# The MLP of a fused transformer layer as half-array matmuls through the scores' banks, and a first batch whose embedding is summed tile by tile

## The reference

```python
B, S, E = 4, 512, 1024                      # batches, positions, width
h = sum over 8 shards of W[s][clip(x - 1575*s, 0, 1574)] + 8*bias + pos_emb
qkv = layernorm(h) @ w_qkv.T                # 32 query heads, 8 key/value heads, 128 wide
probs = softmax(causal(q k^T / sqrt(128)))
h = h + (probs @ v) @ w_dense.T
t = layernorm(h)[:, perm].reshape(-1, 16, 64)          # 16 heads of 64
t = gelu(einsum('bhd,hdm->bhm', t, up))                # 64 -> 256, per head, exact gelu
out = h + einsum('bhm,hmd->bhd', t, down).reshape(-1, 1024)[:, unperm]
```

## Time and profile before

| | us |
|---|---|
| median of 3 runs (lowest to highest) | 2775.52 (2774.55 to 2777.88) |
| the profiled execution: its time | 2776.71 |
| its span on the core | 2774.9 |
| TensorE matmul busy | 2656.9 |
| ScalarE, VectorE, GpSimd busy | 1333.4, 1304.2, 1035.6 |

### The profile page before, as it was taken

How to read it: one execution, slowest core, us unless ns; L and a number is a source line. 1 busy time by engine, 2 the same in 40 slices (tenths; PEclk the granted TensorE clock), 3 DMA queues, 4 the chain that set the end, 5 groups by cost and what they waited for, 6 DMA issues and landing times.

```text
span 2774.9 us, 36350 instructions
## 1 busy us (share of the span) xinstructions
PE 2656.9 (96%) x13040; PEld 2192.2 (79%) x13040; DVE 1304.2 (47%) x3181; ACT 1333.4 (48%) x3209; POOL 1035.6 (37%) x822
## 2 busy tenths in 40 slices
PE   3999999999999999999999999999999999999988
PEld 2788888888878888887887888888787888888863
DVE  4444444554544444455453544446445445444441
ACT  2544444444455555445445555544545555554422
POOL 3333334333244444433334444443333444443311
PEclk9999999999999999999999999999999999999999
DMA  5222224222222222522222223342232222222230
GB/s 131 64 70 73 69 76 119 80 71 71 87 77 83 89 79 77 143 69 69 89 74 74 88 80 91 94 112 76 61 99 73 77 80 88 81 87 73 72 114 31
DMA packets 116556, 229.85 MB, mean 83 GB/s; under 512 B 13837, under 2 KB 13837, under 8 KB 116282
## 3 DMA queue, kind: packets, MB, share of 16 engines
q1 hardware_dynamic: 108954, 202.36, 24.6%
q0 software_dynamic: 7424, 25.17, 3.6%
HBM read 210.70 MB, written 16.78 MB: 82 GB/s over the span
## 4 chain that ended last, share of the span: by engine, by line
PE 87%; ACT 6%; DVE 4%; issue 1%; DMA 1%; POOL 0%; SPq 0%; ACTq 0%; DVEq 0%; POOLq 0%
PE fb L413 22%; PE fb L415 22%; PE fb L414 22%; PE tp L432 4%; PE sc L413 2%; PE sc L414 2%; PE sc L415 2%; PE pv L415 2%; PE pv L413 2%; PE pv L414 2%; ACT w_hi L592 1%; PE fb L469 1%; PE fb L571 1%; PE sc L423 1%; PE fb L564 1%
## 5 line engine op out<-in xcount | busy, mean ns | idle before, releaser
L882 POOL TENSOR_TENSOR w_lo<-w_raw,w_hi 128x512 fp32r<-128x512 f32 x688 | 883.1, 1303 | 1452.8 <-ACT w_hi L592 1451.3
L413 PE MATMUL fb<-xn_hi,w_hi 128*128 128x512 f32 x1536 | 607.7, 396 | 20.1 <-ACT g_raw L683 8.8
L592 ACT ACTIVATE w_hi<-w_raw 128x512 fp32r<-128x512 f32 x688 | 410.7, 631 | 408.2 <-PE fb L415 378.0
L415 PE MATMUL fb<-xn_hi,w_lo 128*128 128x512 f32 x1536 | 600.1, 391 | 0.0
L414 PE MATMUL fb<-xn_lo,w_hi 128*128 128x512 f32 x1536 | 599.7, 390 | 0.0
L413 PE MATMUL fb<-at_hi,w_hi 128*128 128x512 f32 x992 | 393.4, 397 | 8.2 <-DVE hacc L784 6.1
L608 ACT ACTIVATE prob<-sc,neg_max 128x128 f32<-128x128 f32 (+3 forms) x512 | 263.4, 527 | 282.2 <-DVE neg_max L743 281.3
L415 PE MATMUL fb<-at_hi,w_lo 128*128 128x512 f32 x992 | 387.6, 391 | 0.0
L414 PE MATMUL fb<-at_lo,w_hi 128*128 128x512 f32 x992 | 386.5, 390 | 0.0
L413 PEld LDWEIGHTS fb<-xn_hi,w_hi 128*128 128x128 f32 x1536 | 288.8, 188 | 91.6 <-ACT g_raw L683 14.0
L415 PEld LDWEIGHTS fb<-xn_hi,w_lo 128*128 128x128 f32 x1536 | 288.7, 188 | 62.1
(11 more groups left out here) (141 smaller groups left out, 3836.7 us busy)
## 6 DMA issues: line engine op xcount, KB each, us to landing
w_raw<-in_w_qkv SPq DMA_DIRECT2D x384, 256.0 KB, 2.8
w_raw<-in_w_dense SPq DMA_DIRECT2D x256, 256.0 KB, 2.6
h_tok<-in_pos SPq DMA_DIRECT2D x16, 512.0 KB, 5.6
h_rows<-hacc SPq DMA_DIRECT2D x32, 256.0 KB, 2.5
w_raw<-in_w_up SPq DMA_DIRECT2D x24, 256.0 KB
w_raw<-in_w_down SPq DMA_DIRECT2D x24, 256.0 KB, 2.5
end_up<-in_w_up SPq DMA_DIRECT2D x8, 256.0 KB, 5.1
end_down<-in_w_down SPq DMA_DIRECT2D x8, 256.0 KB, 5.2
```

The lines of the kernel that those rows point to most:

```text
L413: pe.matmul(dst, a_hi, b_hi, start=first, stop=False)
L415: return pe.matmul(dst, a_lo, b_hi, start=False, stop=last)
L592: act.activation(w_hi[:, m % RW, :], w_raw[:, m % RAW, :], copy).then_inc(w_rounded, 1)
L882: pool.tensor_tensor(w_lo[:, m % RW, :], w_raw[:, m % RAW, :], w_hi[:, m % RW, :], ALU.subtract)\
```

## The change

- In the loop the MLP no longer uses `product`. `mlp_w` holds raw f32 weights of a pair, up and down side by side (128x512, one DMA for each pair, issued by SP at step F). U is one plain f32 matmul over 64 partitions (one head, one half of the rows of the array), heads taking turns; O is four plain f32 matmuls with 64 output columns, heads taking turns between the lower and upper 64 partitions of one `fb` bank. The steps R, `y_hi`, `y_lo`, `g_hi`, `g_lo`, and the 48 weight tiles of up and down with their `w_hi` and `w_lo`, are gone.
- U's results go to the three banks of `sc` (the scores') in turn, no longer to `fb`; scores wait for the Gelus before them, a pair's first U for the exponentials before it. In the unit's order the four U stand in two groups of two.
- The end: the same forms; U goes through six banks (`sc`, `tp`, `pv`).
- The start: positions go to `first_pos` (in the space of `at_hi`/`at_lo`), the gathers don't wait for them and no longer add by DMA; POOL adds the positions tile by tile (step J); TensorE adds `h_tok` into the bank by an identity matmul; DVE takes statistics from the bank and ACT copies it back. Edge rows are loaded from ACT's queue, `coef` is made for batch 0 first and for the rest after K, statistics and scales are taken tile by tile, normalised tiles take turns in `row_buf` and `prob`, and the first eleven weight splits move from ahead of START into the X steps and Q0.

```diff
-MLP = ("S0 N0 Q2 q D0 Ta0 f D1 Tb0 S1 N1 Q3 D2 Ta1 D3 Tb1 S2 p F D4 D5 N2 D6 r D7 u0 PV0 u1 Ta2 u2 Q0 u3 Tb2 S3 P N3 "
-       "PV1 o R K Ta3 U0 PV2 U1 Tb3 U2 Q1 U3 V PV3 VT")
+MLP = ("S0 N0 Q2 q D0 Ta0 f D1 Tb0 S1 N1 Q3 D2 Ta1 D3 Tb1 S2 p F D4 D5 N2 D6 D7 u0 u1 PV0 u2 u3 Ta2 Q0 Tb2 S3 P N3 "
+       "PV1 o K U0 U1 Ta3 PV2 U2 U3 Q1 Tb3 V PV3 VT")
-START = "A G0 G1 G2 G3 B0 B1 B2 B3 B4 B5 B6 B7 La Lb X0 X1 X2 X3 X4 X5 X6 X7 Q0 K Q1 V VT"
+START = ("A G0 G1 G2 G3 J0 J1 J2 J3 B0 B1 La0 B2 Lb0 B3 La1 B4 Lb1 X0 X1 B5 La2 B6 Lb2 X2 X3 B7 La3 Lb3 X4 X5 X6 X7 "
+         "Q0 K Q1 V VT")
+        for m in range(RW):
+            first = Step("X", 0, 0, min(m // 2 * 2 + 1, 7)) if m < 8 else Step("Q", 0, 0, 0)
+            self.splits[first].append(m)
+        def up_bank(s):
+            if s.kind == "U":
+                return sc[:, (4 * PAIRS * s.b + s.i) % 3, :]
+            return (sc[:, 0, :], sc[:, 1, :], sc[:, 2, :], tp[:, 0, :], tp[:, 1, :], pv[:, :])[s.i % 6]
+            positions(first_pos)
...
+                if s.kind == "F":
+                    n = PAIRS * s.b + s.i
+                    if n > 1:
+                        sp.wait_ge(job_full, full(Step("O", (n - 2) // PAIRS, 0, (n - 2) % PAIRS)))
+                    sp.dma_start(mlp_w[:, n % 2, :], w_mlp[s.i]).then_inc(mlp_in[n % 2], 16)
...
+                if tally.ups[s] > 0:
+                    pe.wait_ge(g_done, tally.ups[s])
                 pe.matmul(sc[:, 0, 0:P], q_first[:, q, :], k_first[:, :], start=True, stop=True)
...
+            def up(dst, w, weight, rows, done):
+                own, cols = slice(DH * (w % 2), DH * (w % 2) + DH), slice(w // 2 * P, w // 2 * P + P)
+                pe.matmul(dst, weight[own, cols], rows[own, :], start=True, stop=True).then_inc(done, 1)
+            def down(s, ready, before, weight, act_of):
+                dst = start_job(s)
+                for w in range(4):
+                    h, m = w % 2, w // 2
+                    pe.wait_ge(ready, before + w + 1)
+                    at = MH + (2 * h + m) * DH
+                    mm = pe.matmul(dst[h * DH:(h + 1) * DH, :], weight[:, at:at + DH], act_of(w),
+                                   start=m == 0, stop=m == 1)
                 mm.then_inc(job_full, 1)
...
+                    if s.b == 0:
+                        pe.wait_ge(h_placed, c + 1)
+                        mm = pe.matmul(dst, ident[:, :], h_tok[:, c, half * S:(half + 1) * S], start=False, stop=True)
...
+                    if w == 0:
+                        pe.wait_ge(mlp_in[n % 2], 16 * (n // 2 + 1))
+                        pe.wait_ge(scaled, n + 1)
+                        pe.wait_ge(exp_done, 4 * tally.scores[s])
+                    if tally.ups[s] > 2:
+                        pe.wait_ge(g_done, tally.ups[s] - 2)
+                    up(up_bank(s), w, mlp_w[:, n % 2, :], y[:, n % 2, :], up_full)
...
+                elif s.kind == "B" and s.b == 0:
+                    act.wait_ge(h_stats, s.i + 1)
+                    act.activation(h_tok[:, c, half * S:(half + 1) * S], fb[:, bank(s), :], copy)\
+                       .then_inc(bank_free[bank(s)], 1)
...
-                    act.activation(g_raw[:, w % 2, :], fb[:, bank(s), :], ACT.Gelu).then_inc(bank_free[bank(s)], 1)
-                    act.activation(g_hi[:, w, :], g_raw[:, w % 2, :], copy).then_inc(g_rounded, 1)
+                    act.wait_ge(up_full, 4 * n + w + 1)
+                    act.activation(g[:, w, :], up_bank(s), ACT.Gelu).then_inc(g_done, 1)
...
+                    if s == Step("K", 0, 0, 0):
+                        dve.wait_ge(x_row_in, 64)
+                        coefficients(S, B * S).then_inc(coef_rest, 1)
...
+                elif s.kind == "J":
+                    pool.wait_ge(pos_in[s.i], 16)
+                    pool.wait_ge(gathered[s.i], 16)
+                    pool.tensor_tensor(h_tok[:, s.i, :], h_tok[:, s.i, :], first_pos[:, s.i, :], ALU.add)\
+                        .then_inc(h_placed, 1)
```

More of the change, by code:

```diff
@@ L170, in __init__, with tower_kernel @@
             self.splits[STEPS[place]].append(m)
-def tower_kernel(nc, x_cols, x_row, table, bias, pos, edge_cols, w_qkv, w_dense, w_up, w_down, perm_cols, out):
+        self.ups, self.scores, ups, scores = {}, {}, 0, 0
+        for s in STEPS:
+            self.ups[s], self.scores[s] = ups, scores
+            ups += s.kind == "U"
+            scores += s.kind == "S"
+        self.la = {s: n for n, s in enumerate(s for s in STEPS if s.kind == "La")}
+def tower_kernel(nc, x_cols, x_row, table, bias, pos, edge_cols, w_qkv, w_dense, w_mlp, perm_cols, out):
     scratch = nc.dram_tensor("h1_rows", [E, S], F32).ap()
-    weights = {"qkv": w_qkv, "dense": w_dense, "up": w_up, "down": w_down}
+    weights = {"qkv": w_qkv, "dense": w_dense}
     tally = Tally()
@@ L301, in tower_kernel @@
         selected = sem("selected")
[L302 to L304 removed]
+        coef_rest = sem("coef_rest")
+        pos_in = [sem(f"pos_in{c}") for c in range(TT)]
+        gathered = [sem(f"gathered{c}") for c in range(TT)]
+        h_placed = sem("h_placed")
+        h_stats = sem("h_stats")
+        h_moments = sem("h_moments")
+        var_step = sem("var_step")
+        shift_done = sem("shift_done")
         rstd_done = sem("rstd_done")
@@ L369, in _ @@
                 sp.dma_start(edge_consts[at, :], edge_cols).then_inc(const_in, 16)
[L370 to L381, removed]
+                token_row(at, 0, S, const_in)
+            positions(first_pos)
             for m in range(RAW):
                 load(m)
-            for m in range(RW):
-                sp.wait_ge(w_ready, m + 1)
-                load(m + RAW)
+            sp.dma_start(perm[:, :], perm_cols).then_inc(x_row_in, 16)
+            for part in range(3):
+                token_row(slice(32 * part, 32 * part + 32), S, B * S, x_row_in)
             for s in STEPS:
@@ L391, in _ @@
                     sp.wait_ge(job_full, full(Step("O", s.b - 2, 0, PAIRS - 1) if s.b > 1 else Step("H", 0, 0, 7)))
-                    for c in range(TT):
-                        sp.dma_start(h_tok[:, c, :], pos[c * P:(c + 1) * P, :]).then_inc(pos_in, 16)
+                    positions(h_tok)
                 if s.kind == "D" and s.g == G - 1:
@@ L533, in _ @@
                     dst = start_job(s)
-                    pe.matmul(dst, ones[:, :], hp[:, 0, :] if s.i else y_raw[:, :], start=True, stop=True)\
+                    pe.matmul(dst, ones[:, :], hp[:, 0, :] if s.i else y[:, 0, :], start=True, stop=True)\
                         .then_inc(job_full, 1)
@@ L588, in _ @@
             copy = ACT.Copy
+            act.wait_ge(zeroed, 1)
+            shards = table.rearrange("(s v) e -> s v e", v=VS)
+            n = SHARDS - 1
+            for part in range(3):
+                at = 32 * part
+                act.dma_start(row_buf[at:at + n, :], shards[0:n, VS - 1, :]).then_inc(edge_in, 16)
+                act.dma_start(row_buf[at + n:at + 2 * n, :], shards[1:SHARDS, 0, :]).then_inc(edge_in, 16)
+                act.dma_start(row_buf[at + 2 * n:at + EDGE, :], bias.partition_broadcast(SHARDS)).then_inc(edge_in, 16)
             def split(m):
@@ L819, in _ @@
+                    dve.bn_stats(stats[:, c, half, :], at if s.b > 0 else fb[:, bank(s), :]).then_inc(h_stats, 1)
                     if half == 1:
-                        dve.wait_ge(h_step, 15 * s.b + (3 * c + 2))
-                        dve.sem_inc(apart, 1)
-                        dve.bn_aggr(moments[:, c, :], stats[:, c, :, :]).then_inc(h_step, 1)
+                        dve.wait_ge(h_stats, 8 * s.b + s.i + 1)
+                        dve.bn_aggr(moments[:, c, :], stats[:, c, :, :]).then_inc(h_moments, 1)
```

281 lines of the change are left out of this document (124 added, 157 removed).

## The result

The changed kernel takes 2689.99 us (median of three runs, 2688.89 to 2691.08) against 2775.52 before: a ratio of 0.969, 95% interval 0.967 to 0.971, 85.5 us less. The forecast was 2718, 57.5 less, with a range of 2672 to 2770. So sign and range held, and the gain was half as large again as forecast. The profiled span is 2689.3 us against 2774.9.

What follows compares the result with a forecast made beforehand. TensorE, busy 96% and carrying 87% of the chain that ended last, was taken as the bound. 2776.7 - 24 (loop) - 19 (start) - 14 (end) = 2719.7 us profiled, 2718.5 against the median; predicted 2718, range 2672 to 2770.

Steps and rivals of the forecast that it cites:

- Slots: Loop, U and O on TensorE: half-array matmuls overlap partly, 11 slots of 0.43 us a pair, 4.75 us.
- the forecast's main case: Loop and end: half pairs, with changes between whole and half array priced; 2700 to 2735 us, chance 0.42.
- rival 2: Loop and end: full pairs, each half streaming by itself, 8 slots, 4.45 us a pair with changes; 2679 us, chance 0.17.
- Changes of form: Loop, TensorE: six changes a pair between whole and half array, 0.165 us each, 1.0 us a pair.
- The stall removed: Loop, the four U: 1.2 us of stall a pair, on an `fb` bank still held by Gelu, goes away.
- New waits in the loop: Loop: U's waits for exponentials and scores' waits for Gelus cost nothing; U3's Gelu wait bounded at 1 us for each of 12 units.
- Start: Start, batch 0: Q0 at about 41.5 us instead of 60.69, 19 us earlier; gain 15 to 25.
- End: End part, 8 pairs: a pair takes 5.8 us instead of 7.68, 14 us saved in all.
- Rival 5: End part: the clock might fall to the low level, +4 us a pair, 2749 us; chance 0.10 shared with start unmoved.

Runs made afterwards that it cites:

- experiment 1: Changed kernel with both U matmuls of a group in the same half of the array and O's four in order A, A, B, B: 2733.97 us.
- experiment 2: Changed kernel with U and O as plain f32 matmuls over the whole array, 128 rows and 128 columns, as many of them, heads mixed: 2763.0 us.
- experiment 3: Changed kernel with O placed behind K, directly ahead of the U group, in the MLP units: 2689.71 us.
- experiment 4: Changed kernel with GpSimd's adds of the positions in the start cut to one column, so the first batch lacks nearly all its positions: 2680.91 us.
- experiment 5: Changed kernel with the positions added by VectorE instead of GpSimd, the last two tiles between the first sums, nothing left out: 2682.64 us.

## Why the prediction was right, and where it was not

**Slots: the step that failed.** "The next matmul, in the other half, is behind them both and can start only beside the second": 11 slots a pair, 4.75 us. The records show eight: both halves' first records start together, and in experiment 1 even when two matmuls of the other half stand between. The row that led there (every record starts after the one before it in the program) held only because every matmul of before used the whole array. It was no evidence on two halves. This was the forecast's main case (chance 0.42); what happened is rival 2 (0.17). The term is 3.44 instead of 4.75, and as 24 x 1.3 = 31 us it is nearly all of what the loop gained over the forecast (35).

**Changes of form: right.** Forecast were 1.0 us a pair, 0.165 each. Measured 1.1 by experiments 1 and 2, and 0.15 to 0.2 for one change by experiment 3; the nearer row (0.085, format alone) would have been too low. The rule that the forecast names from the Trainium skill ("TensorEngine Tiling (Array Packing)", Key Properties), the drain at a change of mode, agrees with the runs, which give the price. Together: rival 2 had 4.45 us a pair. Slots and changes as measured are 3.44 + 1.1 = 4.54; the unit distances show 4.32, the MID unit's wait accounting for the difference.

**The stall removed: Gelu was only part of it.** The forecast put 1.2 us a pair, 2.4 a unit, down to banks held by Gelu. The two waits for Gelu in a unit are 0.56 and 0.73, 1.3 together. A third one in every MLP unit is for VectorE's low part of a projection (TensorE's timeline of before):

```profile
840.55 0.50 PE L413 MATMUL fb<-xn_hi,w_hi 128*128 128x512 f32 x1 [0.66 <-DVE q_lo L773]
```

It is gone too: in the loop TensorE waited 9.1 us for such low parts before and 1.1 after. The three make 1.95 a unit; what the rest was stays open.

**New waits in the loop: right.** TensorE's waits in the changed kernel from 700 to 2580 us, in total, times and longest:

```profile
PE fb L435 <- DVE hacc L830: 5.0, 12, 0.4
PE tp L456 <- DVE pt_lo L795: 3.9, 10, 0.7
PE tp L456 <- DVE prob L791: 3.9, 3, 1.3
```

These are the three largest. None in the whole list is for an exponential or a Gelu, and in 1880 us they are small change.

**Start: a term mis-sized.** The forecast had the edge rows done at 13.5 from instructions priced as in before, where GpSimd only issued its gathers beside them. They were done at 24.6, which makes 10.4 of the 13.3 us by which Q0 (54.84) missed 41.5. Shown by experiment 4. A sign of it stood in the rows: coef took 6.68 us in before, which was read as the instruction's own length. Beside it ran GpSimd's `w_lo` (first line, from before); in the changed kernel a quarter of coef alone took 0.54, and the rest, forecast at 5.0, is the second line:

```profile
21.86 5.48 POOL L882 TENSOR_TENSOR w_lo<-w_raw,w_hi 128x512 fp32r<-128x512 f32 x4
```

```profile
70.73 1.07 DVE L748 TENSOR_SCALAR coef<-hacc,edge_consts 96x1536 bf16<-96x1536 int32 x1
```

The other 2.9 us vary with the clock: from first matmul to Q0 27.2 were forecast, 30.1 measured in the first profile and 27.7 in the second; experiment 5 has 29.8, and the same start with TensorE kept busy 26.1. ScalarE's list of operations was sized about right, 19.3 us busy from 25 to 55 us against 20.4; that it is the limit there is not shown, since ScalarE was idle for a third of that time.

**End: right in its chain, one term too large.** Forecast for a pair: O 2.15, VectorE's chain 2.07, U 1.3 and changes 0.3. Measured from 2642.56 to 2647.68: 1.87, 2.19 and 1.06. The first and last term are slots again. Rival 5 is out: from 2644 to 2676 us the granted clock is 1.00. Seven times 2.57 less is 18 of the 22 us; the rest lies ahead of the first pair (2.5) and behind the last (1.3).

**Sum.** The forecast missed by 35 in the loop and 8 in the end to one side and by 14 in the start to the other. Without the miss in the start the time would have been 2676, just inside the range: that the forecast missed by only 28.5 us is in part luck, two errors of opposite sign. Rival 2, full pairs with the start as forecast, gave 2679; with the start that was measured it gives 2693, 3 us from 2690.

## What to carry to other kernels

Two plain f32 matmuls on different halves of TensorE's array cost the time of one, in both orders tried here, as long as both halves have work queued; price each change between whole array, row halves and column halves at some 0.2 us and keep what shares a form together. Don't put a long elementwise instruction of GpSimd beside VectorE instructions that somebody waits for: here VectorE's instruction ended only when GpSimd's did. And before calling an order of rows a rule, ask whether any row could have shown the opposite.

## What the runs showed of the hardware

- Two streams: O's eight records on column halves start within 1.3 us also in the order A, A, B, B (experiment 1, where four matmuls take four slots). A plain f32 matmul of 512 columns is two records of 0.43 us.
- A change of form costs 0.15 to 0.2 us, between row halves and column halves too; a change only between plain f32 and fp32r in the whole array cost nothing that could be seen (experiment 2: 1.72 us for four slots).
- A GpSimd add of two 128 x 1024 f32 tiles (2.97 us) stretched VectorE's casts beside it from 0.68 to 2.71 us and a subtraction of 32 x 1024 from 1.22 to 3.24.
- The granted clock in a stretch where TensorE is busy 3.0 of 5 us differs between executions of one program (0.70 and 1.00 from 35 to 40 us). Idle matmuls that filled the gaps held it at 1.00 and were worth 5.5 us of time.
